# Placing one-time weight steps inside hand-written engine orders: a two-layer gated attention and MoE kernel

## What is computed

```
x = x + tanh(g_xattn[0]) * L0_xattn(ctx, ctx, layernorm(x))   # 16 heads of 8, softmax over the HEADS axis
x = x + tanh(g_ffn[0])   * L0_ffn(layernorm(x))               # 8 experts of 256, top 2, all experts computed
x = x + tanh(g_xattn[1]) * L1_xattn(layernorm(x), ctx)        # bidirectional attention flow, W_l of 4*128
x = x + tanh(g_ffn[1])   * L1_ffn(layernorm(x))               # ternary weights, 8-bit activations, INNER 512
```

## Time and profile before

| what | value |
|---|---|
| runs | 432.39, 435.32, 439.3 us; median 435.32 |
| profiled execution, own time | 432.61 us |
| its span, first to last instruction | 430.8 us, mean granted TensorE clock 0.953 |
| busy PE / VectorE (DVE) / GpSimd (POOL) / ScalarE (ACT) | 317.4 / 328.7 / 285.2 / 238.5 us |
| DMA | 24.03 MB in 34214 packets, mean 56 GB/s |

### The profile page before, as it was taken

The page is one execution under the profiler, slowest core; times in us unless marked ns, Lnnn a source line. Parts: engine busy times, 40 slices in busy tenths (PEclk is TensorE's granted clock), DMA queues, the critical chain, the costliest instruction groups (busy, mean ns, idle before and its releaser), DMA issues. The chain is left out here.

```text
span 430.8 us, 9908 instructions
## 1 busy us (share of the span) xinstructions
PE 317.4 (74%) x3106; PEld 275.4 (64%) x3106; DVE 328.7 (76%) x1003; ACT 238.5 (55%) x630; POOL 285.2 (66%) x440
## 2 busy tenths in 40 slices
PE   0133348889888888898998898878879978984622
PEld 0122236778787777777887797768768867873501
DVE  1467445968778999999899989997989877785233
ACT  3503314534574679468847865785558647645434
POOL 4145877788889698789869897888686934231100
PEclk9999999999899999999999999999999999996555
DMA  5672410430141024003400430034000100100000
GB/s 169 187 201 71 115 59 2 118 92 2 41 123 48 2 68 138 6 0 88 135 4 2 124 97 2 2 98 114 3 11 2 38 2 2 38 2 1 12 0 12
DMA packets 34214, 24.03 MB, mean 56 GB/s; under 512 B 3570, under 2 KB 31860, under 8 KB 34164
## 3 DMA queue, kind: packets, MB, share of 16 engines
q1 hardware_dynamic: 33444, 23.22, 18.9%
q10 hardware_dynamic: 720, 0.20, 0.2%
HBM read 16.07 MB, written 7.34 MB: 54 GB/s over the span
## 5 line engine op out<-in xcount | busy, mean ns | idle before, releaser
L816 PE MATMUL ps_z<-m_xhi,w_hi 128*128 128x256 f32 x256 | 81.1, 317 | 14.9 <-DVE m_h L1141 8.3
L620 POOL TENSOR_TENSOR attn<-attn,head_inv 128x1024 f32<-128x1024 f32 x32 | 75.7, 2369 | 2.3 <-DVE head_inv L1116 2.3
L698 ACT ACTIVATE m_tanh<-ps_z 128x256 f32<-128x256 f32 x128 | 48.6, 383 | 46.7 <-PE ps_z L818 46.6
L817 PE MATMUL ps_z<-m_xhi,w_lo 128*128 128x256 f32 x256 | 73.2, 286 | 0.0
L1009 PE MATMUL ps_d<-wdn,m_h 128*128 128x128 f32 x512 | 70.8, 281 | 3.3 <-DVE m_h L1141 1.3
L818 PE MATMUL ps_z<-m_xlo,w_hi 128*128 128x256 f32 x256 | 73.1, 285 | 0.0
L1009 PEld LDWEIGHTS ps_d<-wdn,m_h 128*128 128x128 f32 x512 | 62.2, 191 | 6.7 <-issue 3.0
L567 POOL TENSOR_TENSOR m_h<-m_u,m_z 128x256 f32<-128x256 f32 x56 | 41.1, 735 | 37.6 <-DVE m_u L1133 37.6
L1133 DVE SCALAR_TENSOR_TENSOR m_u<-m_tanh,ps_z 128x256 f32<-128x256 f32 x128 | 53.1, 415 | 15.0 <-ACT m_tanh L698 13.4
L816 PEld LDWEIGHTS ps_z<-m_xhi,w_hi 128*128 128x128 f32 x256 | 49.5, 193 | 22.1 <-DVE m_u L1133 8.7
L614 POOL TENSOR_TENSOR tree<-tree 128x256 f32<-128x256 f32 (+2 forms) x96 | 48.5, 505 | 7.5
(11 more groups left out here) (205 smaller groups left out, 762.2 us busy)
## 6 DMA issues: line engine op xcount, KB each, us to landing
rows_dram<-qk_parts SPq DMA_DIRECT2D x16, 192.0 KB, 2.1
k_rows<-rows_dram SPq DMA_DIRECT2D x16, 192.0 KB
q_rows<-rows_dram SPq DMA_DIRECT2D x16, 192.0 KB
w_raw<-in_w SPq DMA_DIRECT2D x2, 1024.0 KB, 6.8
rows_dram<-qk_parts SPq DMA_DIRECT2D x16, 128.0 KB, 1.8
x_in<-in_x SPq DMA_DIRECT2D x8, 128.0 KB, 2.2
...
```

The costliest lines, as they stand in the source:

```text
L620: pool.tensor_tensor(e, e, head_inv[:, u % 2].unsqueeze(1).to_broadcast([P, HEADS, HALF]), ALU.mult).then_inc(s_attn, 1)
L698: act.activation(m_tanh[:, k % 2], ps_z[k % 2][:, 0:TOK], ACT.Tanh, scale=0.5).then_inc(s_mt, 1)
L816: pe.matmul(dst, hi_w, hi_x, start=start, stop=False)
L817: pe.matmul(dst, lo_w, hi_x, start=False, stop=False)
```

## The change

1. Tables. `AT`, `FIRST`, `LAST` and `START` go; `WHEN` gives a place for each step and each pair by itself, and `ONCE` one for each one-time weight step. All orders of all engines are new. The numbers only rank the steps, as before.
2. The one-time steps are steps of their own (`sp.w_out`, `sp.w_moe`, `sp.w_fin`, `sp.w_ffn`, `sp.w_late`, `act.qkv_hi`, `act.w_hi` in four halves, `act.gate_hi`, `act.th`, `pool.w_lo` and `dve.w_lo` in two halves each, `pe.w_total`, `dve.w_small`, `dve.w_abs`, `dve.w_scale`, `dve.w_round`, `dve.w_clip`, ...), with waits at their users.
3. The keys' product stands ahead of the transpose of the queries' input: kq.0 waits for ct_lo and for v_diag of the pair before, a_xt for the keys' rest, kq.1 for a_xlo.
4. ct_hi and ct_lo have two buffers; their writers wait for the values' product of two pairs before.
5. Head sums u = 1 and 3 of pair 0 are one tensor_reduce each on VectorE instead of a tree of four levels on GpSimd.

```diff
+SUM_DVE = {0: (1, 3)}
+WHEN = { ... }   # one row per step, eight places
+ONCE = { "sp.w_moe": 341, "sp.w_out": 106, "sp.w_fin": 798, "sp.w_ffn": 1127, "sp.w_late": 1745, ... }
...
             for now in order("sp"):
+                if due(now, "sp.w_moe"):
+                    sp.wait_ge(w_attn, 80)
+                    sp.wait_ge(ld_a, 32)
...
+                if due(now, "sp.w_late"):
+                    sp.dma_start(wdn[:], ...).then_inc(w_late, 16)
+                    sp.dma_start(wl[:], ...).then_inc(w_late, 16)
...
-                    wait(pool, s_v, p.before().count(1, 1))
-                    pool.tensor_tensor(ct_lo[:], ct_in[:], ct_hi[:].bitcast(F32), ALU.subtract).then_inc(s_ctlo, 1)
+                    wait(pool, s_v, p.before(2).count(1, 1))
+                    pool.tensor_tensor(ct_lo[:, p.c % 2], ct_in[:], ct_hi[:, p.c % 2].bitcast(F32),
+                                       ALU.subtract).then_inc(s_ctlo, 1)
...
-                if p := due(now, "pool.head_sum", u):
+                if (p := due(now, "pool.head_sum", u)) and u not in SUM_DVE.get(p.c, ()):
...
+                for k in range(4):
+                    if due(now, "act.w_hi", k):
+                        n, half = k % 2, slice((k // 2) * HALF_W, (k // 2 + 1) * HALF_W)
+                        act.wait_ge(w_moe, 48)
+                        act.activation(w01_hi[:, n, half], w01_raw[:, n, half],
+                                       ACT.Copy).then_inc(c_hi1 if n else c_hi0, 1)
...
                 if p := due(now, "pe.a_xt"):
                     pe.wait_ge(s_axn, p.count(2, 2))
-                    wait(pe, s_vd, p.before().count(2, 2))
+                    pe.wait_ge(s_rest[0], p.count(1, 1))
...
                 if p := due(now, "pe.kq", 0):
                     pe.wait_ge(s_ctlo, p.count(1, 1))
-                    pe.wait_ge(s_axlo, p.count(1, 1))
+                    wait(pe, s_vd, p.before().count(2, 2))
...
                 if p := due(now, "pe.kq", 1):
-                    pe.wait_ge(s_rest[0], p.count(1, 1))
+                    pe.wait_ge(s_axlo, p.count(1, 1))
...
                     if p := due(now, "pe.up", k):
+                        if p.first and k in (0, TILES // 2):
+                            half = 1 if k else 0
+                            pe.wait_ge(c_hi0, half + 1)
+                            pe.wait_ge(c_mlo, half + 1)
+                            pe.wait_ge(c_mlo1, half + 1)
...
+                for n in range(2):
+                    if due(now, "dve.w_lo", n):
+                        half = slice(n * HALF_W, (n + 1) * HALF_W)
+                        dve.wait_ge(c_hi0, n + 1)
+                        dve.tensor_tensor(w01_lo[:, 0, half], w01_raw[:, 0, half], w01_hi[:, 0, half].bitcast(F32),
+                                          ALU.subtract).then_inc(c_mlo, 1)
...
+                    if (p := due(now, "dve.head_sum", u)) and u in SUM_DVE.get(p.c, ()):
+                        b, k0 = u // 2, HALF * (u % 2)
+                        dve.wait_ge(s_exp, p.count(4, u + 1))
+                        wait(dve, s_hinv, p.count(4, u - 1))
+                        e = attn[:, b, :, k0:k0 + HALF]
+                        dve.tensor_reduce(tree[:, u % 2, 14], e.rearrange("p h k -> p k h"), AX.X,
+                                          ALU.add).then_inc(s_hsum, 1)
```

More of the change, by code:

```diff
@@ new lines @@
+ONCE = {
+    "sp.w_moe": 341,
+    "sp.w_out": 106,
+    "sp.w_fin": 798,
+    "sp.w_ffn": 1127,
+    "sp.w_late": 1745,
+    "act.qkv_hi": 406,
+    "act.w_hi": (1398, 1206, 1493, 1302),
+    "act.gate_hi": 1626,
+    "act.th": 918,
+    "pool.w_lo": (1324, 2176),
+    "pe.w_total": 2284,
+    "dve.qkv_scale": 421,
+    "dve.qkv_lo": 506,
+    "dve.w_lo": (1556, 6521),
+    "dve.gate_lo": 1668,
+    "dve.w_small": 1130,
+    "dve.w_abs": 2105,
+    "dve.w_scale": 2381,
+    "dve.w_round": (2555, 2595, 2634),
+    "dve.w_clip": (2685, 2785),
+}
@@ L165, in rows, with sums @@
         return slice(self.c, self.c + 1)
-def place(table, step, n):
-    at = table.get(step, 0)
-    return at[n] if isinstance(at, tuple) else at
 def order(engine):
     steps = []
-    for step, at in AT.items():
+    for step, at in WHEN.items():
         if step.startswith(engine + "."):
-            for n in range(len(at) if isinstance(at, tuple) else 1):
-                for c in range(PAIRS):
-                    when = START[c] + place(AT, step, n)
-                    if c == 0:
-                        when += place(FIRST, step, n)
-                    if c == PAIRS - 1:
-                        when += place(LAST, step, n)
-                    steps.append((when, step, n, c))
+            for n, times in enumerate(at if isinstance(at[0], tuple) else (at,)):
+                steps += [(when, step, n, c) for c, when in enumerate(times)]
+    for step, at in ONCE.items():
+        if step.startswith(engine + "."):
+            for n, when in enumerate(at if isinstance(at, tuple) else (at,)):
+                steps.append((when, step, n, 0))
     return [(step, n, c) for _, step, n, c in sorted(steps)]
+def sums(c, u, dve):
+    before = [(a, b) for a in range(PAIRS) for b in range(4) if (a, b) < (c, u) and (b in SUM_DVE.get(a, ())) == dve]
+    return len(before) + 1
 def due(now, step, n=0):
@@ L615, in _ @@
                             if n > 1:
-                                pool.wait_ge(s_tree, p.count(16, 4 * u + lvl))
+                                pool.wait_ge(s_tree, 4 * sums(p.c, u, False) - 4 + lvl)
                             src, at, n = dst, at + n, n // 2
@@ L732, in _ @@
                     act.wait_ge(s_fct, p.count(1, 1))
+                    if p.first:
+                        act.wait_ge(w_fin, 112)
                     wait(act, s_fz, p.before().count(1, 1))
@@ L774, in _ @@
                     act.wait_ge(s_fq2, p.count(1, 1))
+                    if p.first:
+                        act.wait_ge(w_late, 32)
                     wait(act, s_fz, p.before().count(1, 1))
@@ L894, in _ @@
                         pe.matmul(ps_a[:, s], ones[0:1], bv_row[:], start=True, stop=False)
-                        last = split_product(ps_a[:, s], ct_hi[:, s], ct_lo[:, s], wqkv_hi[:, 2], wqkv_lo[:, 2],
+                        last = split_product(ps_a[:, s], ct_hi[:, p.c % 2, s], ct_lo[:, p.c % 2, s], wqkv_hi[:, 2], wqkv_lo[:, 2],
                                              start=False)
@@ L955, in _ @@
                         pe.wait_ge(s_gqs, p.count(1, 1))
+                        if p.first and u == 0:
+                            pe.wait_ge(c_wr, 5)
                         wait(pe, s_gp, p.count(4, u))
@@ new lines, in _ @@
+                for n in range(3):
+                    if due(now, "dve.w_round", n):
+                        dve.wait_ge(c_wm, 2)
+                        dve.tensor_scalar(wf_r[:, n], wf_raw[:, n], wscale[:, n:n + 1], ROUND, ALU.mult,
+                                          ALU.add).then_inc(c_wr, 1)
+                if due(now, "dve.w_clip", 0):
+                    dve.wait_ge(c_wr, 3)
+                    dve.tensor_scalar(wf_t[:], wf_r[:], ROUND, 1.0, ALU.subtract, ALU.min).then_inc(c_wr, 1)
```

469 lines of the change are left out of this document (272 added, 197 removed), and 138 rows, old and new, of the table WHEN.

## The result

The changed kernel is slower: median 440.88 us (439.29 to 448.2) against 433.93 (432.39 to 439.3) of the kernel before, measured beside it. The ratio is 1.0131 with a 95% interval from 1.0081 to 1.0181, so 1.3% slower, clear of noise. I had forecast 424.0 and a range up to 434. The profiled execution took 441.02, its span is 439.2 at a mean clock of 0.935 (before 430.8 at 0.953).

The account below looks back on a forecast made before the run. VectorE was taken to bound the middle (38.68 of 41 us, 94%), chains of waits the start and end. 3.5 + 7.0 - 0.5 - 1.0 = 9.0 us off the profiled 432.61 gave 423.6, taken as 424.0; range 414 to 434.

Parts of the forecast that it names:

- Gain A: Start, first scores: earlier stores and fetches bring the first head_max from 33.55 to 30.0, gaining 3.5 us (bounds 0 and 4.9).
- each about 0.45 us to issue: Start, SP's queue: the issue time assumed for each DMA of SP.
- With all parts ready before SP comes to them, the bytes decide: Start: DMA bytes set the first scores; 13.0 + 2.9 + 5.3 + 7.0 = 28.2, so head_max near 30.
- The Trainium skill's rule that I had weighed: Start: descriptors of one issuing engine's row are consumed in ring order, which speaks against w_late ahead of the rows.
- Gain B: First pair's attention: 5.0 us off GpSimd's run plus 2.0 behind the last norm, 7.0 us gained (bounds 4 and 8).
- Loss C: Pair 0's MoE: half of w_lo moves there on VectorE and PE's up 8 waits; 0.5 us lost (bounds 0 and 3).
- The middle at nothing: Middle pairs: new orders and doubled ct buffers change 0 us; bounds 2.3 us a pair better, 1.5 worse.
- The new orders move single steps by a place or two on each engine; VectorE's work per pair is the same: Middle pairs: reordering is small and leaves VectorE's work unchanged, so 0 us was taken.
- VectorE's 38.68 us per 41 cover them, and if that cover went PE (36.33) would be next: Middle pairs: VectorE's busy time hides keys-first and the doubled ct buffers, both at nothing; PE the next limit.
- Keys ahead of queries at nothing: Middle pairs: the ps_a steps form one chain of the same length in both orders, so 0 us.
- Loss D: End, last pair: g_down.1 and out.1 come between f_z and x3, losing 1.0 us (bounds 0.5 and 1.5).
- The fourth: Rival, MoE stretches: VectorE and PE take turns waiting; two such waits, 3.1 us a pair, give 442.6; chance 0.08.

Follow-up runs that it names:

- run 10: run 1's version with the seven w_fin DMAs, load_f@0 and w_late issued behind pair 0's fetches, VectorE's small weight step later: 431.73 us, ratio 0.9909.
- run 9: Changed kernel with w_late issued behind the fetches of pair 0 and w_out behind w_moe: 439.78 us, ratio 1.0129.
- Run 8: Changed kernel with all four head sums of pair 0 on GpSimd again: 446.8 us, ratio 1.0272.
- run 1: Changed kernel's start up to the first m_stats, then the previous kernel's orders and old key/query waits (old middle): 428.43 us, ratio 0.9877.
- the filled changed kernel: Changed kernel with ten unread products on PE behind m_xt of each pair but the first: 438.46 us, ratio 1.0105.
- run 6: Ten unread products on PE behind m_xt of each pair but the first: 426.62 us on run 1's version, 438.46 us on the changed kernel.
- run 7: The filled changed kernel with act.f_an of pair 2 moved ahead of o_t@4 on ScalarE: 436.93 us, ratio 1.0056.
- run 4: Changed kernel, but from pair 2 on old waits and queries' a_xt ahead of the keys, key stores and parts behind: 442.0 us, ratio 1.0146.
- run 2: run 1's version with keys ahead of queries in the old middle orders, new waits holding: 437.4 us, ratio 1.0121.
- run 3: run 2's version with ct_hi beside a_norm and ct_lo right behind m_rstd: 431.52 us, ratio 0.9880.

## Why the prediction was wrong, and where it was right

- *Gain A, 3.5 us: wrong, -1.6.* The first step that failed is the price of SP's issues, "each about 0.45 us to issue". At 0.45 the 17 issues from the first store to the last fetch would have ended at 21.8; they took 0.83 each (one store 1.35, wl 1.57, a fetch 0.64 to 0.78) and ended at 28.15. So the second failed too, "With all parts ready before SP comes to them, the bytes decide": its sum has the fetches through at 28.2, when the last was only issued, and the scores came 7.0 us behind that (before 6.6). Eleven DMAs out of the way brought the scores to 28.0 (run 10). Whether SP's own time or the bytes made the issues long isn't shown: the DMA engines' share was 1.02 from 16 to 20 and 1.06 from 25 to 28. The Trainium skill's rule that I had weighed, in DMA: Bandwidth & Descriptors (Queues, rings and completion order), shows next to no effect here: from the last fetch's issue to the scores 7.0 us with w_late ahead in the ring, 6.8 without (run 9).
- *Gain B, 7.0 us: right*, 34.3 to 27.3, by its own terms: GpSimd's run 18.5 for 18.8, 5.2 behind the last norm for 4.9. The head sum was mis-sized, 1.92 us and not 1.2, inside the bounds and covered. Run 8 puts 5.2 us on the two sums.
- *Loss C, 0.5 us: the term was mis-sized.* In pair 0, m_xlo to the end of its MoE took 38.8 us, before 35.8: 3.0, my upper bound. In run 1, where the old orders and w_lo.1 ahead of the MoE came together, it is 35.5; so how much of the 3.0 is w_lo and how much the orders isn't told apart. The moved half took 2.10 us, its twin at 18.56, with GpSimd idle, 1.21. The timeline of both engines at the moved half:

```profile
76.58 2.10 DVE L1300 TENSOR_TENSOR w_lo<-w_raw,w_hi 128x1024 fp32r<-128x1024 f32 x1
```

```profile
75.22 2.38 POOL L852 TENSOR_TENSOR attn<-attn,head_inv 128x1024 f32<-128x1024 f32 x1
```

  From 76.58 to 77.60 both would run, and w_lo took 0.9 us longer. The Trainium skill, SBUF — State Buffer (Who interferes with whom), says that a VectorE instruction with two SBUF inputs contends with a GpSimd one that reads SBUF; the trace agrees. It also says that a tensor_reduce doesn't contend: the trace agrees in that the tree step of GpSimd that began at 46.10, during the first head sum, took 1.26 us, as others do (the head_norm at 42.95 overlapped that sum by only 0.4 us), and the two head sums took 1.92 and 1.94.
- *The middle at nothing: wrong, and outside its bounds.* +13.6 us in four rows, 3.4 a row, where I had 1.5 at most. Two steps failed. The first is "The new orders move single steps by a place or two on each engine; VectorE's work per pair is the same", from which I took 0. VectorE's busy time for the same 1006 instructions is 337.9 us against 330.6 in run 1: 330 to 331 in all seven versions with the old middle, 337 to 340 in all with the new one and the two sums on VectorE. Part of it are small instructions that took longer while GpSimd had one running. Between 60 and 430 us twelve took over 0.15 us more than the median of their kind, 5.7 us in all; the filled changed kernel has twelve too, with 5.8 us, the kernel before six with 1.8, run 1 seven with 2.1. The longest, and what GpSimd had beside it:

```profile
268.66 1.25 DVE L1523 SCALAR_TENSOR_TENSOR g_sc<-g_amc,cg 128x2 f32<-128x2 f32 x1
```

```profile
268.62 1.27 POOL L846 TENSOR_TENSOR tree<-attn 128x512 f32<-128x512 f32 x1 [2.83 <-ACT attn L944]
```

  In the four rows that is 4.0 us against 0.8 before. No run takes them out, so what they cost in time isn't shown. The second failed step is "VectorE's 38.68 us per 41 cover them, and if that cover went PE (36.33) would be next". It took PE's 36.33 us as a fixed price. It is one only at full clock; the earlier trace rows had a row at 0.96 (100 to 140), and I passed over it. The four rows hold 17 us more of half clock; at 0.25 to 0.45 each that is 4 to 8 of the 13.6 us. That it isn't all shows at equal clock: nine executions of the kernel before at a mean clock of 0.932 took 435.4 to 438.4 us, the changed kernel at 0.934 and 0.935 439.3 and 441.0, with its start 5.5 us ahead. The rest is lost at full clock, in VectorE's longer work and in new waits: 2.9 us in the row from m_stats@4, 2.5 in the row that run 6 cleaned, of which run 7 found 0.5 in one place. Which places in the orders make the others stays open.
- *Keys ahead of queries at nothing*: right for this kernel (run 4), but only because ct_lo is made a pair ahead. In the old orders the same edit costs nine us (run 2), six of them by a wait of PE, behind which half clock stood (run 3).
- *Loss D, 1.0 us*: f_stats@7 to x3@7 took 20.9 us, before 20.6. x3 stands 1.0 us behind f_z, with g_down.1 and out.1 between, as said; f_z itself comes sooner, so 0.3 is lost, below my lower bound of 0.5.

```profile
414.59 0.63 PE L1180 MATMUL ps_f<-wl,f_prod 128*128 128x128 f32 x2
...
415.02 0.63 PE L1212 MATMUL ps_g<-wf_q,g_pt 128*128 128x128 bf16 x4
...
416.18 0.48 DVE L1507 SCALAR_TENSOR_TENSOR x<-ps_f,th,y_res 128x256 f32<-128x256 f32 x1
```

- *Rivals.* The fourth had the right side and nearly the number (442.6). Its mechanism is right in part: VectorE's idle time rose by 2.0 us a row, in waits for PE and ScalarE of up to 1.5 us, where it had 3.1 of them. That the number came so near is luck, since it has nothing of longer VectorE instructions and of the clock. No rival named the clock. The changed tables had told more than I read from them: read as hundredths of a us, their places of m_stats lie 42 to 45.5 us apart from pair 3 on (17265, 21724, 26270, 30610, 34838), those of the old `START`, in thousandths, 39. I had taken both as ranks alone.
